# A transformer kernel of eight stages: shared experts partly behind the routed tiles, earlier gathers, earlier ternary weights, and the routed rows mixed by VectorE

## The reference, cut to what matters

```python
# L1 attention: 8 heads of 32 numbers over ctx; then the L1 feed-forward:
s  = jnp.mean(jnp.abs(w))                       # one number per weight matrix w1, w2, w3
wq = jnp.round(jnp.tanh(w / (s + EPS))) * jnp.arctanh(s)        # ternary weights
h  = silu(linear_bit(x, w1, g1)) * linear_bit(x, w2, g2)        # 1024 hidden numbers
x += linear_bit(h, w3, g3)                      # activations rounded to 8 bit per token

# L2 feed-forward: a causal attention of 16 heads (hid), then experts:
top_w, top_i = top_k(softmax(x2 @ gate_w.T), 4)                 # 16 experts, 4 per token
routed = sum over the 4 of top_w * (silu(x2 @ g_e) * (x2 @ u_e)) @ down_e
shared = silu(x2 @ sg) * (x2 @ su) @ sh_down_w.T                # every token
x += hid + routed + shared

# L3: attention of 16 heads of 128 over ctx, then a feed-forward part with 704 hidden numbers
```

## Time and profile before

| what | value |
|---|---|
| median of 3 runs | 2105.93 us |
| the profiled execution, its own time | 2107.05 us |
| its span in the trace | 2105.3 us (1.75 us lie around it) |
| mean granted TensorE clock | 0.889 of full speed |
| busy share: PE, DVE, ACT, POOL | 77%, 66%, 39%, 30% |

### The profile page before, as it was taken

The page is one execution under the profiler, slowest core; times in us unless marked ns, Lnnn a source line. Parts: engine busy times, 40 slices in busy tenths (PEclk is TensorE's granted clock), DMA queues, the critical chain, the costliest instruction groups (busy, mean ns, idle before and its releaser), DMA issues. The chain is left out here.

```text
span 2105.3 us, 29671 instructions
## 1 busy us (share of the span) xinstructions
PE 1612.0 (77%) x9237; PEld 1138.7 (54%) x9318; DVE 1386.2 (66%) x3775; ACT 815.5 (39%) x2357; POOL 624.6 (30%) x744
## 2 busy tenths in 40 slices
PE   3559988696243888898889599999785995887774
PEld 2324434364121466666666488888653553776763
DVE  6779968587775688888888346455364332567765
...
GB/s 60 105 5 181 195 49 1 1 1 76 33 123 86 311 1 1 1 2 1 1 1 1 176 15 15 1 1 1 17 207 68 89 88 212 93 73 66 63 26 8
DMA packets 104405, 129.33 MB, mean 61 GB/s; under 512 B 14208, under 2 KB 89184, under 8 KB 101056
## 3 DMA queue, kind: packets, MB, share of 16 engines
q1 hardware_dynamic: 95264, 112.39, 16.6%
...
...
## 5 line engine op out<-in xcount | busy, mean ns | idle before, releaser
L580 POOL TENSOR_TENSOR l0f_diag<-g_identb,l0f_mask 128x1024 bf16<-128x1024 bf16 x16 | 32.0, 2023 | 226.4 <-PE l0f_psA L836 209.8
L2750 ACT ACTIVATE l2x_probs<-l2x_psS,l2x_nmax 128x128 f32<-128x128 f32 x256 | 90.7, 371 | 10.2 <-DVE l2x_nmax L2664 9.9
L2534 POOL TENSOR_TENSOR l2x_probs<-l2x_probs,l2x_rtotal 128x512 f32<-128x512 f32 x64 | 66.8, 1043 | 90.2 <-DVE l2x_rtotal L2670 90.2
L3241 DVE COPY moe_xgT<-moe_psX 128x256 f32<-128x256 f32 x47 | 19.9, 424 | 100.1 <-PE moe_psX L3349 100.1
L2545 POOL TENSOR_TENSOR l2x_vsm<-l2x_vraw,l2x_smooth_row 128x512 f32<-128x512 f32 x64 | 84.7, 1344 | 3.7 <-ACT l2x_vraw L2784 3.4
L3110 POOL MEMSET moe_before<- 128x256 f32 x1 | 0.3, 316 | 287.3 <-POOLq L162 287.3
L2072 POOL DMA_INDIRECT l3a_routed<-rows,slots_slot_of x32 | 31.0, 968 | 174.7 <-issue 166.2
L2895 PEld LDWEIGHTS l2x_psS<-l2x_kT,l2x_qT 128*128 128x128 f32 x512 | 66.8, 191 | 21.9 <-issue 17.7
L996 ACT ACTIVATE l1a_probs<-l1a_psS,l1a_nmax 128x256 f32<-128x256 f32 x128 | 58.8, 473 | 43.9 <-PE l1a_psT L1024 37.0
L819 PE MATMUL l0f_psH<-l0f_wT,l0f_xm 128*128 128x512 bf16 x256 | 68.0, 389 | 10.2 <-DVE l0f_h L660 9.0
L921 POOL TENSOR_TENSOR l1a_probs<-l1a_probs,l1a_rtotal 128x512 f32<-128x512 f32 x64 | 65.1, 1039 | 32.7 <-DVE l1a_rtotal L958 32.7
...
## 6 DMA issues: line engine op xcount, KB each, us to landing
...
```

The source lines that it names most:

```text
L2534: nc.gpsimd.tensor_tensor(probs[:, n % 2, :, :], probs[:, n % 2, :, :], rtotal[:, n % 2, :].unsqueeze(2).to_broadcast([P, 4, P]), ALU.mult)\
L2750: last = nc.scalar.activation(probs[:, n % 2, j, :], psS[:, j, :], ACT.Exp, bias=nmax[:, n % 2, j:j + 1], scale=1.0, accum_out=total[:, n ...
```

## The change

**Ternary weights.** A class `TernaryWeights` holds the three matrices and their gains from the start of the L1 attention on. SP loads them there. ScalarE sums their absolute values in three instructions of 128x2048, ahead of half steps 8, 12 and 16 of the L1 attention. In the same stage the clearing of `vs` moves behind the first keys, and the filling to half step 1. In the L1 feed-forward part the thresholds follow the statistics directly, the first ternary matrix comes ahead of `xn`, the third behind the norm of the rows; in the loop, `add(b - 1)` moves from behind `gate(b)` to between `vh` and the wait for `rh`.

**Experts.** 8 shared units run ahead of the tiles and 8 behind them (`AHEAD`); two units go to a routing group. The last stores are waited for by GpSimd, which then gathers the rows of sequences 0 and 1, still in this stage; VectorE mixes sequence 0 at the stage's end.

**L3 attention.** VectorE mixes all other sequences in `stats(b)`; GpSimd only gathers and inverts. `mix_on_gpsimd` is there but is not called.

```diff
-def stage_l1_xattn(nc, G, A):
+H1 = 1024
+
+
+class TernaryWeights:
+
+
+    SUMS_AT = (8, 12, 16)
...
+    def load(self, sp, A):
+        for j, (name, chunks) in enumerate((("L1_w1T", KC), ("L1_w2T", KC), ("L1_w3T", H1 // P))):
+            sp.dma_start(self.w[j][:, :].rearrange("p (c o) -> p c o", c=chunks),
+                         A[name].rearrange("(c p) o -> p c o", p=P)).then_inc(self.loaded[j], 16)
+        sp.dma_start(self.g12[:, 0, :], row(A["L1_ffn_g1"], D)).then_inc(self.gains_loaded, 16)
+        sp.dma_start(self.g12[:, 1, :], row(A["L1_ffn_g2"], D)).then_inc(self.gains_loaded, 16)
+        sp.dma_start(self.g3[:, :], row(A["L1_ffn_g3"], H1)).then_inc(self.gains_loaded, 16)
+        sp.wait_ge(self.gains_loaded, 48)
+
+    def sum(self, nc, act, n):
+        if n in self.SUMS_AT:
+            j = self.SUMS_AT.index(n)
+            act.wait_ge(self.loaded[j], 16)
+            wait(act, self.summed, j)
+            nc.scalar.activation(self.magnitude[:, :], self.w[j][:, :], ACT.Abs, accum_out=self.asum[:, j:j + 1])\
+                .then_inc(self.summed, 1)
+
+
...
-                nc.gpsimd.memset(vs[:, :, :, :, :], 0.0).then_inc(zeroed, 1)
                 nc.gpsimd.memset(parity[:, :], 0.0).then_inc(parity_made, 1)
                 n = 1
                 for h in range(HEADS):
@@ -924,6 +963,7 @@
 
                 keys(0)
                 keys(1)
+                nc.gpsimd.memset(vs[:, :, :, :, :], 0.0).then_inc(zeroed, 1)
```

```diff
                     u = n % 2
+                    V.sum(nc, act, n)
+                    if n == 1:
+                        spread_values()
```

```diff
-                normalise_all(nc, G, T, xn)
-
-                dve.wait_ge(loaded, 96)
-                for j in range(3):
-                    last = nc.vector.tensor_reduce(asum[:, j:j + 1], w[j][:, :], AX.X, ALU.add,
-                                                   apply_absolute_value=True)
-                last.then_inc(summed, 1)
+                for b in range(B):
+                    o.mark(nc.vector.bn_stats(T.stats[:, b, :], G.x[:, b, :]))
+                o.settle()
+                for b in range(B):
+                    o.mark(nc.vector.bn_aggr(T.mv[:, b, :], T.stats[:, b, :]))
+                o.settle()
+                nc.vector.tensor_scalar(T.ve[:, :], T.mv[:, :, 1], 1e-5, None, ALU.add).then_inc(T.var_ready, 1)
                 dve.wait_ge(totals, 1)
...
+                ternary(0)
+                dve.wait_ge(T.rstd_ready, 1)
+                for b in range(B):
+                    last = nc.vector.tensor_scalar(xn[:, b, :], G.x[:, b, :], T.mv[:, b, 0:1], T.rstd[:, b:b + 1],
+                                                   ALU.subtract, ALU.mult)
+                last.then_inc(T.ln_ready, 1)
+                ternary(1)
                 dve.wait_ge(atanh_ready, 1)
                 o.step(nc.vector.tensor_scalar(atanh[:, :], atanh[:, :], 0.5, None, ALU.mult))
                 dve.wait_ge(squared, 1)
                 nc.vector.tensor_scalar(vrms[:, :], ss[:, :], 1.0 / D, eps, ALU.mult, ALU.add).then_inc(ms_ready, 1)
+                ternary(2)
                 dve.wait_ge(rrms_ready, 1)
 
...
+                    if not is_zero(b):
+                        add(b - 1, 1 - u)
                     dve.wait_ge(rh_ready, b + 1)
                     o.step(nc.vector.scalar_tensor_tensor(out=y3[:, :], in0=h[u][:, :], scalar=rh[:, u:u + 1],
                                                           in1=g3[:, :], op0=ALU.mult, op1=ALU.mult))
@@ -1236,8 +1281,6 @@
 
                 def step(b, u, next_one):
                     gate(b, u)
-                    if not is_zero(b):
-                        add(b - 1, 1 - u)
                     if two_follow(b, next_one):
                         first(b + 2, u)
                     quantise_hidden(b, u)
@@ -1250,14 +1293,14 @@
...
             def _(act):
+                act.wait_ge(ratio_ready, 1)
+                nc.scalar.activation(atanh[:, :], ratio[:, :], ACT.Ln).then_inc(atanh_ready, 1)
                 act.wait_ge(T.ln_ready, 1)
                 for b in range(B):
                     last = nc.scalar.activation(square[:, 0:D], xn[:, b, :], ACT.Square, accum_out=ss[:, b:b + 1])
                     last.then_inc(squared_each, 1)
                     act.wait_ge(squared_each, b + 1)
                 nc.scalar.copy(square[:, 0:1], ss[:, 0:1]).then_inc(squared, 1)
-                act.wait_ge(ratio_ready, 1)
-                nc.scalar.activation(atanh[:, :], ratio[:, :], ACT.Ln).then_inc(atanh_ready, 1)
```

```diff
-        STEP = SHARED // GROUPS
+        AHEAD = 2 * 4
+        STEP = AHEAD // GROUPS
...
+        tile_at = lambda m: m - AHEAD if AHEAD <= m < AHEAD + TILES else None
+        result_at = lambda m: m // 2 if m < AHEAD else min(m - AHEAD, TILES) + AHEAD // 2 + max(m - AHEAD - TILES, 0) // 2
+        half_at = lambda m: m if m < AHEAD else m - TILES if m >= AHEAD + TILES else None
...
                                                      x2[:, b, :], None).then_inc(scattered, 16)
+                for u in range(NY):
+                    pool.wait_ge(stored[u], 16 * len(range(u, TILES, NY)))
+                R.gather(G, 0)
+                R.gather(G, 1)
 
...
                             assign(g - 1)
                         if g < GROUPS:
                             compare(g)
+                            break_ties(g)
                         else:
                             list_tiles()
-                    elif j == 1 and g < GROUPS:
-                        break_ties(g)
-                    elif j == 2 and g < GROUPS:
+                    elif g < GROUPS:
                         choose(g)
 
-                for m in range(UNITS + 1):
...
-                    if m >= 3 and m % 2 and m < SHARED + 3:
-                        add_shared((m - 3) // 2)
+                    if m >= 2 and half_at(m - 2) is not None and half_at(m - 2) % 2:
+                        add_shared(m - 2)
+                R.mix_on_vector(dve, G, 0)
 
```

```diff
-                    mix(2)
+                    invert(0)
+                    R.gather(G, 2)
+                    invert(1)
+                    R.gather(G, 3)
                     for b in range(B):
                         if b + 2 < B:
                             invert(b + 2)
                         if b > 0:
                             side.on_gpsimd(pool, G, b - 1)
-                        if b + 3 < B:
-                            mix(b + 3)
+                        if b + 4 < B:
+                            pool.wait_ge(R.mixed_first, b + 3)
+                            R.gather(G, b + 4)
                     side.on_gpsimd(pool, G, B - 1)
...
+                    if b >= 1:
+                        R.mix_on_vector(dve, G, b)
+                    dve.wait_ge(R.mixed_first, b + 1)
                     o.step(nc.vector.bn_stats(T.stats[:, b, :], G.x[:, b, :]))
...
+    def gather(self, G, b):
+        for k in range(TOP2):
+            n = b * TOP2 + k
+            self.nc.gpsimd.indirect_dma_start(self.rows[b % 2][:, k, :], None, G.rows,
+                                              bass.IndirectOffsetOnAxis(ap=G.slot_of[:, n:n + 1], axis=0))\
+                .then_inc(self.gathered[b % 2], 16)
+
+    def mix_on_vector(self, dve, G, b):
+        dve.wait_ge(self.gathered[b % 2], 16 * TOP2 * (b // 2 + 1))
+        for k in range(TOP2):
+            n = b * TOP2 + k
+            ins = self.nc.vector.scalar_tensor_tensor(
+                out=G.x[:, b, :], in0=self.rows[b % 2][:, k, :], scalar=G.weight_of[:, n:n + 1],
+                in1=G.x[:, b, :], op0=ALU.mult, op1=ALU.add)
+            if k < TOP2 - 1:
+                ins.then_inc(self.vorder, 1)
+                dve.wait_ge(self.vorder, (TOP2 - 1) * b + k + 1)
+        ins.then_inc(self.mixed_first, 1)
```

225 lines of the change are left out of this document (103 added, 122 removed).

## The result

| kernel | median us | range, runs |
|---|---|---|
| before | 2104.79 | 2102.1 to 2106.78, 4 |
| changed | 2069.75 | 2065.31 to 2077.96, 4 |

A forecast was written before the change was run, and what follows sets the result against it. No engine is full throughout; each stage is bound by the wait that ends last in it. Terms -1.9 - 14.3 - 18.6 + 0.5 - 2.7 - 8.5 = -45.5, from the median 2105.93, gave 2060.5 us, range 2045 to 2077.

The forecast's parts named there:

- -14.3 at the start of the L1 feed-forward part: L1 feed-forward before its loop: with the new order, the loop's preparation begins at 534.1 and not 548.37, 14.3 us earlier.
- -18.1 for its loop with the barrier: L1 feed-forward loop: moving `add` saves 18.6 us; one more pool to clear before the L2 stage costs 0.5.
- The -9.9 of the experts' head: Router to first tile load: earlier assignment and fewer slot waits let the tiles start 9.9 us earlier.
- the tail costs (+21.5): Experts' stage, first tile load to the L3 stage: eight shared units now follow the tiles, 21.5 us longer.
- the three terms make -2.7: Router to first L3 scores: the L3 start saves 14.3 us, its stage begins 11.6 later, so 2.7 us saved.
- -1.9: L1 attention: moved clearing and copies save 3.1 us, three absolute sums on ScalarE cost 1.2, net 1.9 saved.
- 18.8 us: L3 start: scores begin 18.8 us into the stage instead of 33.1, held by the last of four query weight loads.
- a mix of 2.05 us on VectorE: L3 sequences: 33.59 us plus this mix gives 35.64 instead of 38.18; the stretch saves 8.5 us in all.
- The rival of transfers at the L3 start: L3 start: the chain also waits for `wo` or the second keys, costing 5 to 6 us, 2066; chance 0.15.
- the held loop: L1 feed-forward loop: ScalarE (`sil`) or TensorE ends each step at about 12.5 us, costing 9 us, 2069.5; chance 0.13.
- the scatters: Experts' stage: all 32 scatters stretched like the worst, adding 22.1 us, 2083; chance 0.02.
- the falling clock in all of L3: L3: TensorE's granted clock falls, making the kernel slower; at 0.64 it costs 92 us, 2153; chance 0.02.

The follow-up runs named there:

- the second profile: The changed kernel run again with nothing changed, as the yardstick for the other experiments: 2069.2 us.
- the 12 units: Changed kernel with 12 shared units ahead of the tiles, 4 behind: 2064.3 us; with clearing behind `q` and query weights first too: 2052.0 us.

## Why the prediction was right, and where it was 9 us too low

The mechanism and the sign held, and the two largest terms were right to 1.4 us: -14.3 at the start of the L1 feed-forward part (measured -13.9 and -14.3), and -18.1 for its loop with the barrier (-18.7 and -19.5). `sil` did not take over; putting one call back gave the old period again. The -9.9 of the experts' head looks as good: 9.8 in every later profile with this routing, and 6.5 in the first, where ScalarE's `gated` and then the slots came late. But this agreement is partly luck. The 7.6 us of waits for slots that I let go were read from a profile in which VectorE stood still once for 3.57 us, and against the old order in the same kernel the routing and the split bring 6.6. What the tail costs (+21.5) was measured as +21.2 and +20.3. From the router to the first scores of L3 the three terms make -2.7; measured are +3.6 and +0.8 (258.5 before, then 262.1 and 259.3): this whole part of the change brought nothing. Most of the gain is the L1 feed-forward stage's (32.6 to 33.8 us), the rest the L3 sequences'.

The terms that were off:

- *"`rstd` and so `q` come 3.5 us earlier ... VectorE's statistics are not late then."* `q` came earlier, and the clearing that had been moved ran beside it. I had asked what stands behind the clearing in its queue, and not what runs beside it in its new place. -1.9 became -0.1, and +5.1 in the second profile. The +5.1 is not the clearing's: the clock rose 47.5 us behind the stage's start there, and at 38 us in the first profile and in before's. That the sums cost nothing offset some of the loss.
- *"What is late next is the query weights: the last of four loads."* The resource was right, the instruction was not. It is the second weight, at 12.6 us, with three products ahead of the scores, of which one or two took 3.78 us and not the 2.1 that I had put, because TensorE had waited. 18.8 us became 22.0 and 23.4.
- *"It gets a mix of 2.05 us on VectorE, which I count in full."* The place was right, the size was not: the mix costs 2.5 in its quad (13.45 against 10.96) and 0.9 in the next (9.70 against 8.83), 3.4 together, because TensorE's clock falls in the longer wait. A sequence took 36.2 us and not 35.64 (from one sequence's first scores to the next's, 32.85 without any mix and 37.5 with GpSimd's), and the stretch gained 4 to 7 us and not 8.5.

By the first profile these are 1.8 + 3.2 + 1.9 us, by the second 7.0 + 4.6 + 4.2; the time was 9 over the forecast. Which of them carried how much is not settled: stretches with the same code vary by 5 to 10 us. Taking them away one by one gained 10 (`q`) and 8 us (query weights) in the medians, of which the traces show 1.4 to 3.4 and 4.6 to 6.0 at their places; both with the 12 units gained 17.7.

The rival of transfers at the L3 start was the nearest of the named ones, but with the wrong transfer: `wo` and the second keys were never waited for. The rivals of the held loop, of the scatters and of the falling clock in all of L3 did not come: 0.89 in the changed kernel's window against 0.90 before.
